# A transformer block with routed experts on one core: columns split earlier, slot table in parts, first slots turned ahead, own rows for empty slots, four additions in flight for two

## What is computed

```python
h = layernorm(x) * (1 + ca) + sa                       # per sequence
qkv = rms(h) @ w_qkv.T;  q, k = rms(q), rms(k);  w = exp(k)
y = sigmoid(q) * cumsum(w * v) / (cumsum(w) + 1e-6)
u, g = split(y @ w_swiglu.T)
x = x + ga * (h + (u * silu(g)) @ w_out.T)
h = layernorm(x) * (1 + cb) + sb
gates = softmax of the 2 largest of h @ gate_w         # 8 experts
routed = sum over the 2 chosen experts e of gate_e * (gelu(h @ w1[e] + b1[e]) @ w2[e] + b2[e])
shared = gelu(h @ shared_w1 + shared_b1) @ shared_w2 + shared_b2
x = x + gb * (routed + shared)
```

## Time and profile before

| what | us |
|---|---|
| median of 3 runs | 2062.34 (2059.6 to 2063.73) |
| profiled execution, its own time | 2057.53 |
| its span, first to last instruction | 2055.7 |
| PE busy | 1949.3 (95%) |
| DVE, ACT, POOL busy | 1276.5, 647.0, 432.2 |

### The profile page before, as it was taken

How to read it: one execution, slowest core, us unless ns; L and a number is a source line. 1 busy time by engine, 2 the same in 40 slices (tenths; PEclk the granted TensorE clock), 3 DMA queues, 4 the chain that set the end, 5 groups by cost and what they waited for, 6 DMA issues and landing times.

```text
span 2055.7 us, 26101 instructions
## 1 busy us (share of the span) xinstructions
PE 1949.3 (95%) x9104; PEld 1567.8 (76%) x9104; DVE 1276.5 (62%) x2660; ACT 647.0 (31%) x1318; POOL 432.2 (21%) x315
## 2 busy tenths in 40 slices
PE   7999999979999999998999999999998989899993
PEld 4688888868888888887887787778776757688883
DVE  6677777565545545568266356446567674598883
ACT  3455656612111111111112222121123323255552
POOL 0021000030000000026001011011071620677774
PEclk9999999989999999999999999999999999999997
DMA  5123110141011210124111321221154733588775
GB/s 223 56 84 107 45 52 22 47 133 62 21 41 62 72 62 21 41 92 139 47 62 52 94 64 66 100 103 66 46 187 146 201 109 123 161 144 148 140 138 83
DMA packets 86234, 188.23 MB, mean 92 GB/s; under 512 B 10036, under 2 KB 26804, under 8 KB 81082
## 3 DMA queue, kind: packets, MB, share of 16 engines
q1 hardware_dynamic: 63242, 129.26, 18.8%
q0 software_dynamic: 22864, 57.31, 13.5%
HBM read 116.84 MB, written 70.29 MB: 91 GB/s over the span
## 4 chain that ended last, share of the span: by engine, by line
PE 71%; DVE 15%; DMA 4%; issue 4%; ACT 4%; POOL 0%; another core or an unknown queue 0%; SPq 0%; POOLq 0%; DVEq 0%; ACTq 0%
PE bank L662 11%; PE bank L664 11%; PE bank L663 11%; PE bank L667 8%; PE bank L669 8%; PE bank L668 8%; PE bank L935 3%; DMA out<-o_t,ids_t 2%; DVE x_lo L1297 1%; PE bank L937 1%; PE bank L960 1%; PE bank L959 1%; PE bank L958 1%; PE bank L826 1%; PE bank L922 1%
## 5 line engine op out<-in xcount | busy, mean ns | idle before, releaser
L662 PE MATMUL bank<-x_hi,w_blk 128*128 128x512 f32 x1024 | 405.8, 396 | 21.6 <-DVE x_lo L1297 20.8
L664 PE MATMUL bank<-x_hi,w_blk 128*128 128x512 f32 x1024 | 400.8, 391 | 0.0
L663 PE MATMUL bank<-x_lo,w_blk 128*128 128x512 f32 x1024 | 400.6, 391 | 0.0
L1454 DVE TENSOR_TENSOR s_t<-act_t,bank 128x512 f32<-128x512 f32 x128 | 87.8, 686 | 315.8 <-PE bank L664 300.9
L662 PEld LDWEIGHTS bank<-x_hi,w_blk 128*128 128x128 f32 x1024 | 193.5, 189 | 64.3 <-issue 13.8
L664 PEld LDWEIGHTS bank<-x_hi,w_blk 128*128 128x128 f32 x1024 | 193.5, 189 | 41.3
L1115 ACT ACTIVATE s_hi<-s_t 128x512 fp32r<-128x512 f32 x128 | 81.2, 634 | 456.5 <-DVE s_t L1454 444.5
L663 PEld LDWEIGHTS bank<-x_lo,w_blk 128*128 128x128 f32 x1024 | 193.8, 189 | 38.8
L540 POOL TENSOR_SCALAR w_blk<-raw 128x1536 fp32r<-128x1536 f32 x16 | 23.8, 1485 | 868.5 <-PE bank L669 710.7
L667 PE MATMUL bank<-w_blk,s_hi 128*128 128x512 f32 x512 | 200.6, 392 | 0.0
L669 PE MATMUL bank<-w_blk,s_lo 128*128 128x512 f32 x512 | 199.3, 389 | 0.0
(11 more groups left out here) (246 smaller groups left out, 3619.4 us busy)
## 6 DMA issues: line engine op xcount, KB each, us to landing
x_t<-y_scratch SPq DMA_DIRECT2D x24, 1024.0 KB, 4.9
residual<-r_t SPq DMA_DIRECT2D x16, 1024.0 KB, 4.3
r_t<-residual SPq DMA_DIRECT2D x16, 1024.0 KB
raw<-w_swi POOLq DMA_DIRECT2D x12, 768.0 KB, 4.5
y_scratch<-y_t SPq DMA_DIRECT2D x32, 256.0 KB, 2.7
r_t<-x_tok SPq DMA_DIRECT2D x8, 1024.0 KB
h_rows<-hrow SPq DMA_DIRECT2D x32, 256.0 KB
y_scratch<-hT SPq DMA_DIRECT2D x8, 1024.0 KB, 3.9
```

What stands on the lines that cost most here:

```text
L662: nc.tensor.matmul(dst, w[:, 0, col:col + P], rhs_hi, start=start, stop=False)
L663: nc.tensor.matmul(dst, w[:, 0, col:col + P], rhs_lo, start=False, stop=False)
L664: return nc.tensor.matmul(dst, w[:, 1, col:col + P], rhs_hi, start=False, stop=stop)
L1454: nc.vector.tensor_tensor(s_t[:, s % 2, :], act_t[:, s % 2, :], bank[4 + (2 * s + 1) % 3][:, :], ALU.mult).then_inc(f.s_ok, 1)
```

## The change

1. At the start SP issues the load of the first x rows before those of the modulation weights. ACT and DVE split the first projection weights before they take shift and gain, and PE turns group 1 after the projection `project(0, 1)` in place of before it.
2. DVE's split for the first tile of pass b stands inside the loop at g = 31, after `quotient(29)`.
3. In pass s, gating(6) moves from block (0, 2) to (1, 0), positions(6) from (1, 0) to (2, 0), gating(7) from (2, 1) to (2, 2), positions(7) from (3, 0) to (3, 1). PE's, ACT's and SP's parts move along.
4. `table()` becomes `slots_of_experts()`, `order_of_additions()` and `places()`, at blocks 0, 1 and 2 of tile 4. The turn of the list blocks moves to (5, 3), `lists()` to (6, 0).
5. PE turns slots 0 and 1 before the last `down` of tile 7; DVE splits them before it evacuates that tile. The banks of `slot_turn` and `slot_down` are exchanged.
6. POOL gathers 4 slots, splits two weight pieces, gathers 4, splits two pieces, gathers 3 more (before: 6 slots, four pieces, 2, 2). gather(j + 11) stands before scatter(j).
7. Empty slots get blocks of spare rows of their own and count as neither fresh nor ordered. `NA = 4`: four semaphores, `due_t` entries for the three slots before, SP loads and waits for three of them for each slot. An entry is at least 16, so that while a semaphore is used for the first time its scatter must have landed.

```diff
-        NA = 2
+        NA = 4
...
+            sp.dma_start(xr[:, 0:NSUB, :], rows_of(0, NSUB)).then_inc(xa_in, 16)
             load_wmod(0)
             load_wmod(1)
-            sp.dma_start(xr[:, 0:NSUB, :], rows_of(0, NSUB)).then_inc(xa_in, 16)
...
-            AHEAD = 2
+            AHEAD = 3
...
-            for j in range(4):
-                pool.wait_ge(ffn["s"].dn, NB_S * LAST + 2 + 2 * (j // 2))
+            pool.wait_ge(ffn["s"].dn, NB_S * LAST + 2)
+            for j in range(2):
                 split_piece(R0 + 12 + j)
-                if j < 2:
-                    fetch(R0 + 14 + j)
+                fetch(R0 + 14 + j)
             pool.wait_ge(ffn["s"].dn, NB_S * NT)
             for j in range(NR_0, NR):
                 gather(j)
+            for j in range(2):
+                split_piece(R0 + 14 + j)
...
+                    if (t, s) == (LAST, NB_S + 1):
+                        pe.wait_ge(ffn["s"].act_ok, NB_S * NT)
+                        slot_rows(0)
+                        slot_rows(1)
...
                 if g >= 2:
                     quotient(g - 2)
+                if g == NG - 1:
+                    split(0)
...
             quotient(NG - 2)
-            split(0)
...
-                    if (t, s) == (0, 2):
-                        gating(LAST - 1)
...
                     if (t, s) == (1, 0):
+                        gating(LAST - 1)
...
-                    if (t, s) == (3, 3):
-                        table()
+                    if t == 4 and s < 3:
+                        (slots_of_experts, order_of_additions, places)[s]()
+                if t == LAST:
+                    slot_x(0)
+                    slot_x(1)
...
-                then(nc.vector.tensor_tensor(tab_f[:, 2, :], tab_f[:, 2, :], tab_f[:, 3, :], ALU.max))
+                then(nc.vector.tensor_tensor(tab_f[:, 2, :], tab_f[:, 2, :], tab_f[:, 3, :], ALU.is_gt))
...
+    spare = slots - 2 * n // P
+    list0[E * n:, 0] += P * (1 + np.arange(slots) % spare).repeat(P)
...
-        "dues": wide(np.stack([16 * ((np.arange(slots) - d).clip(0) // 2) for d in (1, 2, 3)]).astype(np.float32)),
+        "dues": wide(np.stack([16 * ((np.arange(slots) - d).clip(0) // 4) for d in (1, 2, 3)]).astype(np.float32)),
```

More of the change, by code:

```diff
@@ L753, in _ @@
                 project(g, 0)
-                if g + 1 < NG:
+                if 0 < g and g + 1 < NG:
                     turn_group(g + 1)
                 project(g, 1)
+                if g == 0:
+                    turn_group(1)
                 if g == 1:
@@ L966, in expert, with shared_tile @@
                 return pe.value_load(tab[0:1, 0, j:j + 1], min_val=0, max_val=E_PLACE[E - 1] * KB // 4)
-            pe.wait_ge(n2.tab_ok, 1)
-            at_e = [expert(j) for j in range(3)]
-            pe.wait_ge(ffn["s"].act_ok, NB_S * NT)
-            slot_rows(0)
-            slot_rows(1)
+            def shared_tile(t):
+                for s in range(NB_S + 2):
+                    if s < NB_S:
+                        up1(t, s)
+                    if (t, s) == (LAST, NB_S + 1):
+                        pe.wait_ge(ffn["s"].act_ok, NB_S * NT)
+                        slot_rows(0)
+                        slot_rows(1)
+                    if s >= 2:
+                        down("s", t, s - 2, w_shr[:, s - 2, :, :], QKV_W, NB_S)
+                    if (t, s) == (0, 1):
+                        logits_to_tokens(LAST - 1)
+                    if (t, s) == (1, 3):
+                        ranks_of(LAST - 1)
+                    if (t, s) == (2, 2):
+                        gates_to_rows(LAST - 1)
+                    if (t, s) in ((0, 4), (0, 5), (1, 0), (1, 1)):
+                        rows_to_hT(LAST, (4, 5, 0, 1).index(s))
+                    if (t, s) == (1, 4):
+                        logits(LAST)
+                    if (t, s) == (2, 0):
+                        logits_to_tokens(LAST)
+                    if (t, s) == (2, 5):
+                        ranks_of(LAST)
+                    if (t, s) == (3, 4):
+                        gates_to_rows(LAST)
+                        pe.wait_ge(n2.gr_ok, LAST)
+                        nc.tensor.matmul(b_x[:, 0:E], mean_w[:, :], prev[:, 0, :], start=True,
+                                         stop=True).then_inc(n2.cnt_mm, 1)
+                    if (t, s) == (5, 3):
+                        pe.wait_ge(lb_in, 16)
+                        for k in range(2):
+                            ins = nc.tensor.transpose(b_x[:, k * P:k * P + NSLOT], lblk[:, :, k],
+                                                      ident_t[0:NSLOT, 0:NSLOT])
+                        ins.then_inc(lb_tr, 1)
+            for t in range(NT):
+                if t == LAST:
+                    pe.wait_ge(n2.tab_ok, 1)
+                    at_e = [expert(j) for j in range(3)]
+                shared_tile(t)
             slot_up(0, at_e[0])
@@ L1704, in _, with slot_x @@
                     evacuate(p, t)
+            bank_x, bank_u, bank_g, bank_o = bank[4:6], bank[6:8], bank[0:2], bank[2:4]
+            def slot_x(j):
+                dve.wait_ge(rt.xh_ok, j + 1)
+                nc.vector.tensor_tensor(xT_lo[:, j % 2, :], bank_x[j % 2][:, :], xT_hi[:, j % 2, :].bitcast(F32),
+                                        ALU.subtract).then_inc(rt.xl_ok, 1)
             def block_s(t, s):
```

99 lines of the change are left out of this document (34 added, 65 removed).

## The result

| | before | after |
|---|---|---|
| median of the runs, us | 2062.39 (2059.6 to 2063.73, 4 runs) | 2028.83 (2027.08 to 2031.01, 4 runs) |
| profiled execution, its own time | 2057.53 | 2031.01 |
| span, granted clock | 2055.7, 0.977 | 2029.2, 0.984 |

The ratio is 0.984, 95% interval 0.9822 to 0.9857: faster by 1.6%. The forecast for the median was 2027.5, and 1.3 us off. For the profiled execution it was 2022.7, and 8.3 us off. Both statements come from the same sum: the profiled execution of before lies 4.9 us under its median, that of after 2.2 over its own, so the profiles differ by 26.5 us and the medians by 33.6.

The account below looks back on a forecast made before the run. PE was taken as the bound: its waits count up to tile 7, POOL's queue from the first gather. Terms +1 - 18 - 3.7 - 11 + 1.3 - 4.4 = -34.8 gave 2022.7 us profiled, 2027.5 median; range 2011 to 2043.

Parts of the forecast that it names:

- Start: x rows loaded ahead of modulation weights: +1 us, from -4 to +3; DVE's head start not used.
- Last group: Pass b's first tile, x_lo split before POOL's work: PE's wait and half clock go, -18 us, between -19 and -13.
- Gating: Pass s, gating(6) moved: PE's waits for prev go, a new wait of about 3 us in tile 1; -3.7 us.
- Table: Slot table cut in three parts in tile 4: PE's wait and half clock there go, -11 us, from -13 to -7.
- the old loss: What the evacuation of tile 3 lost to POOL's contention before the change; its going was counted as -1.5 us.
- the step "+1.5": POOL's list and weight work now contends in tile 3, costing as much as that tile's evacuation lost before: +1.5 us.
- the wait moves on: Rival: s_lo contention behind the early split +5, tiles 1 and 3 at half clock +5, end +3; 2041 us, 19%.
- Routed stage: From scatter 0 to scatter 70: -4.4 us, to some 262 us.
- its four lines: Scatter 0 to 4 +6.1, seven ordered slots +9.8, the other 48 -3, scatter 59 to 70 -17.3 us.
- The term of the extra loads: Seven ordered slots: two more SP loads follow the landing, 1.4 us each slot, +9.8 us in all.
- The first rival: Extra loads are done while SP waits anyway and POOL ends at its own pace; 2012 us, 20%.
- the slower rival: SP becomes the bound: at 1.2 us a load a slot takes 3.7, +42, so 2069 us; 3%.

Follow-up runs that it names:

- loads ahead: Changed kernel, but SP loads all three due entries of a slot before the first of its waits; 2017.82 us, ratio 0.9778.
- the run with the split late: Changed kernel, but DVE's four x_lo of pass b's first tile stand behind quotient(30) again; 2046.25 us, ratio 0.9915.
- raised semaphores: Changed kernel with SP's loads before its waits and each of four addition semaphores raised once early by a one-row copy; 2012.96 us, ratio 0.9756.
- two-in-flight: Changed kernel with two additions in flight in place of four, one due-entry load per slot; 2022.39 us, ratio 0.9796.
- all-together: Changed kernel with SP's loads before its waits, semaphores raised early, POOL's weight pieces spread and the start as before the change; 2011.62 us, ratio 0.9745.
- the run with the pieces spread: Changed kernel, but POOL's eight expert-weight pieces of tiles 3 to 5 are spread over the second halves of tiles 3 to 6; 2031.41 us, ratio 0.9852.

## Why the prediction was right, and where it was not

**The reading was right**: PE's waits up to tile 7, POOL's queue from there. It is confirmed from both sides. The first slots that PE turns ahead are worth nothing that can be told from noise (2031.57 without), and what shortens POOL's queue (12.0 us from scatter 0 to 70 with the loads ahead) comes out at the end (-11.0).

**Start**: direction and size right (+1 forecast, +1.3 measured). The 1.2 us more by 320 us lie within what equal code shows from one execution to the next.

**Last group**: -16 against -18. The missing 2 us fit the wait of 2.5 for `s_t` ahead of 451, which is not there when PE comes later (the run with the split late). The prediction named `quotient(30)` and the first `s_t` and `s_lo` as late next and called them covered, and for the first 40 us they were. But POOL stretched the next three `s_lo` to 2.63, 3.35 and 3.88 us. Behind the third, DVE went on without a pause from 433.18 to 451, with the last group's quotient, the gains and the norm's statistics, and only then came the `s_t`.

**Gating**: -4.0 against -3.7, with its parts. The new wait in tile 1, forecast at about 3 us, is 3.28 us. The half clock behind it, +2 in the forecast, came in this execution and not in all (see the last section).

**Table**: the one mis-sized term, -5.6 against -11. Its main part was even better than forecast (tile 4: -13.1; forecast -11 and -1.5 for the old loss). What failed is the step "+1.5" for POOL's list and weight work in tile 3. It measured 7.5, because I took the size from the evacuation that the old order disturbed. In the new order the splitting meets `x_lo`, the evacuation, two `s_lo` and then the positions, all ahead of one `s_lo` that PE waits for, and a wait of 4.5 us brings half clock with it. The prediction's rival "the wait moves on" had this mechanism, half clock in tiles 1 and 3, at +5 for the two together.

**Routed stage**: -5.6 against -4.4, and each of its four lines within 2.5 us. The term of the extra loads was taken at 1.4 us an ordered slot; with the loads ahead of the waits the steps fell by 1.2 on average (0.7 to 2.4 each). Behind the landing, in the changed kernel, the loads start 0.6 to 0.7 us apart (four of them from 1804.0 to 1805.9). The first rival (the loads cost nothing) is refuted by that run, since only their place was changed. The price that the Trainium skill gives for such a load (DMA: Bandwidth & Descriptors, "Latency and other measured facts", a floor of about 600 ns) would give 1.2 us for two, and the run agrees with it better than with the 1.4 that I took from the loop of the earlier trace rows.

That SP becomes the bound, the slower rival, did not happen: steps without order stayed at 3.3 us. The signs that the prediction gave for being right are all there: no wait in tile 4, ordered slots at 7.40, the first four steps at 5.8 to 7.2, the last eleven at 2.07, and 260.6 us from scatter 0 to 70.

**The range.** That the median came within 1.3 us is partly luck: the terms as profiled miss by 8.3 us, and 7 of these were given back by how the two profiled executions lie to their medians. The range of 2011 to 2043 covers both.

## What to carry over

Where a queue waits for a landing and then reads what it needs to go on, put the reads ahead of the wait: here that was worth 11 us, and without it a deeper flight was a loss. For work that is moved beside another engine's, size the contention from everything that stands between there and the next thing that the bounding engine waits for, not from the idle time of the tile. A gain on an engine that only runs ahead of a slower queue can be hidden, as that of the first slots was here, so look first at who issues without a pause.

## What the runs showed of the hardware

How long POOL's gather takes hangs on what DVE does when it starts. In four kernels (before, after, loads ahead, raised semaphores) I compared each gather's start between 1765 and 1990 us with DVE's `o_t` and `gb_row`, both with two inputs in SBUF. Of the 71 that start outside them, 70 take 0.96 to 1.00 us (the last 1.04); of the 159 that start at least 0.05 us into one, most take 1.1 to 1.5, with 1.25 the commonest. The ends say why. With the two-in-flight and the all-together kernels added, 208 gathers start 0.1 to 0.6 us into a `gb_row` or `o_t`, and every one ends 0.83 to 0.89 us after that DVE instruction has ended: the gather does not get on until DVE is done. It is not ACT and not DVE work in general: 13 gathers of these kernels that start in a `p_t` but in neither DVE instruction take 0.99 at most, and 70 that start in another DVE instruction (each with a PSUM input) 1.04 at most.

This locks the two engines: POOL, which could go at 3.19 us a slot, goes at DVE's and PE's 3.45 for as long as the gather falls there. In the run with raised semaphores the steps without a wait were 7.7 us longer in all than with the loads ahead alone. The Trainium skill (SBUF — State Buffer, "Who interferes with whom") has the contention of such DVE instructions with GpSimd instructions that read SBUF, and infers that generating descriptors isn't hit by them. These gathers, which also take their row numbers `ids_t` from SBUF, are lengthened all the same, mostly by 0.26 us, and the measurement decides. Whether it is the reading of the row numbers or the descriptors that is held up, no run here shows.

Two SP loads with their waits after a landing took 1.2 us, and four additions of 128 rows in flight end at 2.1 us each, against 2.8 with two in flight and 7.0 one after the other (5.6 in the kernel before, without the two loads behind the landing).

A wait of PE can cost more than its length, since the granted clock can fall to half behind it. Tiles of 24.3 us became 31.4 with one wait of 3.9, 32.4 with one of 4.5 and 36.6 with one of 9.7: 2.6 to 3.6 us on top of each. With the one of 2.8 in the run with the pieces spread, half clock lasted into the next tile, and the two tiles together lost 9.4 us, 6.6 on top. But it need not fall. Tile 1 of pass s has the same wait of about 3.3 us in nearly all these kernels; the changed kernel and the one with raised semaphores:

```profile
1561.02 0.80 PE L672 MATMUL bank<-w_shr,s_hi 128*128 128x512 f32 x1 [3.28 <-DVE s_lo L1734]
...
1562.22 0.50 PE L675 MATMUL bank<-w_shr,s_hi 128*128 128x512 f32 x1 [3.25 <-DVE s_lo L1737]
```

Behind the first the granted clock is 0.50 (1563 to 1566 us) and the tile takes 36.2 us, behind the second it stays at 1.00 and the tile takes 33.5. Seven executions go the first way, six the second. So what a wait of this length costs can't be had from one profile.
